# Splitting x1 and h into f16 parts before the transpose instead of after it

## The reference

```
q, k = rope(bf16(x Wq.T)), rope(bf16(x Wk.T))          # one head of 256
o    = sum over the allowed keys of exp(q k.T / 16)    # one number per row
x1   = layernorm(x + relu(o fc1_w.T + fc1_b) fc2_w.T + fc2_b)
```

```
xa = x1 P_w.T                         # 64 numbers per row
C1, C2, C3 = top3_softmax(xa U1.T), top3_softmax(xa U2.T), top3_softmax(xa U3.T)
h  = gelu(sum_e C1[:, e] (x1 W1[e].T))
y  = sum_e C2[:, e] (h W2[e].T) + C3 b2
return layernorm(x1 + y)
```

## Time and profile before

| | |
|---|---|
| median of 3 runs | 327.04 us (326.6 to 327.73) |
| the profiled execution | 327.78 us, of which its span is 325.9 us |
| granted TensorE clock over the span, mean | 0.973 of full speed |
| busy: PE, DVE, ACT, POOL | 284.7, 256.9, 155.6, 115.3 us |
| first mixture of group k's pass 2 starts, k = 0 to 5 | 132.22, 158.42, 184.46, 210.48, 236.52, 262.39 us |
| first mixture of passes 3, 0, 1 and 2 after the one at 184.29 us | 190.92, 197.61, 202.93, 210.32 us |

### The profile page before, as it was taken

The page is one execution under the profiler, slowest core; times in us unless marked ns, Lnnn a source line. Parts: engine busy times, 40 slices in busy tenths (PEclk is TensorE's granted clock), DMA queues, the critical chain, the costliest instruction groups (busy, mean ns, idle before and its releaser), DMA issues.

```text
span 325.9 us, 6342 instructions
## 1 busy us (share of the span) xinstructions
PE 284.7 (87%) x1978; PEld 191.6 (59%) x1978; DVE 256.9 (79%) x849; ACT 155.6 (48%) x327; POOL 115.3 (35%) x264
## 2 busy tenths in 40 slices
PE   0999999979854988999999899899899997999981
PEld 0444455444323667676677577668577566667771
DVE  0069789999976479689889979988988987997672
ACT  1137747655661371435635544634743663634231
POOL 1000018999999102141332431332323314133221
PEclk9999999998995999999999999999999999999997
DMA  8999999700000000000010000000000010010111
GB/s 230 413 411 218 202 187 186 114 2 0 0 1 0 3 2 0 16 20 18 16 35 16 18 16 27 26 18 19 23 27 19 18 32 19 17 34 19 31 33 37
DMA packets 19235, 20.58 MB, mean 63 GB/s; under 512 B 1600, under 2 KB 18432, under 8 KB 18688
## 3 DMA queue, kind: packets, MB, share of 16 engines
q1 hardware_dynamic: 18480, 19.22, 24.2%
q10 hardware_dynamic: 720, 0.93, 1.0%
HBM read 15.94 MB, written 4.19 MB: 62 GB/s over the span
## 4 chain that ended last, share of the span: by engine, by line
PE 35%; DVE 32%; POOL 16%; issue 7%; ACT 6%; DMA 2%; ACTq 0%; DVEq 0%; POOLq 0%
PE bank L830 20%; DVE early L1188 11%; PE bank L686 9%; POOL W L380 5%; POOL wtmp L377 4%; POOL W L379 3%; DVE st L1225 3%; DVE stats L1036 2%; DVE early L1230 2%; POOL rstd L389 2%; DVE top L1057 2%; DMA gatew<-in_gate 2%; ACT x L546 2%; DVE zrest L1068 2%; PE bank L782 2%
## 5 line engine op out<-in xcount | busy, mean ns | idle before, releaser
L830 PE MATMUL bank<-W,early 128*128 (+1 forms) x630 | 75.6, 273 | 6.3 <-DVE early L1188 4.0
L830 PE MATMUL bank<-W,x1T 128*128 (+1 forms) x630 | 77.3, 278 | 0.5 <-DVE early L1188 0.3
L686 PE MATMUL bank<-early,wqk 128*128 128x512 f32 x128 | 65.1, 642 | 8.6 <-DMA gatew<-in_gate 8.6
L830 PEld LDWEIGHTS bank<-W,x1T 128*128 128x128 f16 x630 | 60.5, 99 | 19.9 <-DVE early L1188 9.5
L830 PEld LDWEIGHTS bank<-W,early 128*128 128x128 f16 x630 | 59.5, 98 | 18.2 <-issue 6.0
L1188 DVE SCALAR_TENSOR_TENSOR early<-bank,Csel,early 128x256 f32<-128x256 f32 x124 | 59.4, 479 | 11.6 <-PE bank L830 7.0
L455 POOL TENSOR_SCALAR ve<-mv 128x1 f32<-128x1 f32 x32 | 7.3, 229 | 120.4 <-DVE mv L1226 120.4
L686 PEld LDWEIGHTS bank<-early,wqk 128*128 128x128 f32 x128 | 23.7, 201 | 30.6 <-issue 21.4
L602 ACT ACTIVATE early<-early 128x256 f32<-128x256 f32 x32 | 13.3, 417 | 50.1 <-DVE early L1188 49.9
L497 ACT ACTIVATE qk<-bank 128x512 bf16<-128x512 f32 x32 | 19.0, 594 | 36.7 <-PE bank L686 36.4
L597 ACT ACTIVATE early<-bank,Csel 128x256 f32<-128x256 f32 x31 | 14.6, 472 | 31.0 <-PE bank L830 30.7
(11 more groups left out here) (105 smaller groups left out, 434.0 us busy)
## 6 DMA issues: line engine op xcount, KB each, us to landing
early<-in_xT SPq DMA_DIRECT2D x16, 256.0 KB, 9.4
xs<-in_x SPq DMA_DIRECT2D x32, 128.0 KB, 7.2
out<-early SPq DMA_DIRECT2D x32, 128.0 KB
W<-in_w1T SPq DMA_DIRECT2D x1, 2048.0 KB, 12.1
W<-in_w2T SPq DMA_DIRECT2D x1, 2048.0 KB, 12.3
W<-in_w1T SPq DMA_DIRECT2D x1, 1024.0 KB, 7.7
W<-in_w2T SPq DMA_DIRECT2D x1, 1024.0 KB, 13.8
wqk<-in_wqkT ACTq DMA_DIRECT2D x1, 512.0 KB, 3.9
```

What stands on the lines that cost most here:

```text
L686: mm = pe.matmul(bank[PROJ[n % 2]][:, :], wqk[:, k, g, :], xTb[:, c % 4, k, :, :].rearrange("p s n -> p (s n)"), start=(k == 0), stop=(k = ...
L830: mm = pe.matmul(where[:, 0:DIM], lhs(hx, c), w, start=(k == 0), stop=(k == 5))
```

## The change

The two f16 parts are made in row layout, and the parts are transposed as f16.

- x1: `normed` on ScalarE is followed, after each two tiles, by a cast of these from SBUF into the new tile `xh` (L577 of the changed kernel). `x1_low` becomes a subtraction of two SBUF tiles into `xh`. For groups 0 and 1, in the early stage, VectorE does it; in the main loop GpSimd does (L403), in pass 2 for both halves of the group. TensorE transposes eight f16 blocks instead of four f32 ones (L783). ScalarE copies the bank to `x1T` as 1024 f16 elements per partition (`x1T_copy`, L582) instead of casting 512; nothing is left for VectorE behind the transpose.
- h: after `gelu`, ScalarE casts with the scale into `hh` (`h_high`, L636), and GpSimd scales h in f32 (`hs`, L408) and subtracts (L410) (`h_low`). TensorE transposes four f16 blocks (L960) instead of two f32 ones, and ScalarE copies 512 f16 elements (`hT_copy`, L640). VectorE's L1230 goes.
- TensorE's transpose of h stands behind the side work of its pass instead of ahead of it. On ScalarE `hT_copy` stands behind both parts of the side work.
- GpSimd does `h_low` of tile i-1 ahead of the factors of the final norm of tile i-2, in every pass, and in pass 2 behind `x1_low` of the first half.
- ScalarE makes an f16 identity once (`identh`).

The diff, cut to what differs in the main path:

```diff
...
+        hh = early[:, 2560:3072].bitcast(F16).rearrange("p (r l n) -> p r l n", r=2, l=2)
+        hs = early[:, 3072:3584].rearrange("p (r n) -> p r n", r=2)
...
+            def x1_low(g, h):
+                pool.wait_ge(xhi_done, 2 * g + h + 1)
+                pool.tensor_tensor(xh[:, h, :, 1, :], x1[:, g % 3, 2 * h:2 * h + 2, :], xh[:, h, :, 0, :], ALU.subtract)\
+                    .then_inc(xlo_done, 1)
+
+            def h_low(t):
+                pool.wait_ge(gelu_done, t + 1)
+                link(pool.tensor_scalar(hs[:, t % 2, :], hact[:, t % 2, :], ipow2[:, 1:2], 0.0, ALU.mult, ALU.add))
+                pool.wait_ge(hhi_done, t + 1)
+                pool.tensor_tensor(hh[:, t % 2, 1, :], hs[:, t % 2, :], hh[:, t % 2, 0, :], ALU.subtract).then_inc(hlo_done, 1)
...
-                if (s, pos) == (2, 1) and group(k + 1):
-                    chosen_exps(k + 1)
+                if (s, pos) == (2, 0) and group(k + 2):
+                    x1_low(k + 2, 0)
+                if (s, pos) == (2, 1):
+                    if group(k + 1):
+                        chosen_exps(k + 1)
+                    if group(k + 2):
+                        x1_low(k + 2, 1)
...
                 aux(k, s, 0)
+                if 1 <= i <= NT:
+                    h_low(i - 1)
...
                 n.then_inc(x1_done, 1)
-
-            def x1_high(g, h):
+                act.wait_ge(x1_done, 2 * g + h + 1)
+                wait(act, x1T_done, 2 * (g - 1) + h + 1)
+                act.activation(xh[:, h, :, 0, :], x1[:, g % 3, 2 * h:2 * h + 2, :], ACT.Copy).then_inc(xhi_done, 1)
+
+            def x1T_copy(g, h):
                 act.wait_ge(x1T_done, 2 * g + h + 1)
                 t = GT * g + 2 * h
-                act.activation(x1T[:, t:t + 2, 0, :, :].rearrange("p t c n -> p t (c n)"),
-                               bank[XPOSE][:, :].rearrange("p (t n) -> p t n", t=2), ACT.Copy).then_inc(x1hi_done, 1)
+                act.activation(x1T[:, t:t + 2, :, :, :].rearrange("p t l c n -> p (t l c n)"),
+                               bank[XPOSE][:, :].bitcast(F16), ACT.Copy).then_inc(x1T_copied, 1)
...
+            def h_high(t):
+                act.wait_ge(gelu_done, t + 1)
                 wait(act, hT_done, t - 1)
+                act.activation(hh[:, t % 2, 0, :], hact[:, t % 2, :], ACT.Copy, scale=ipow2[:, 1:2]).then_inc(hhi_done, 1)
+
+            def hT_copy(t):
+                act.wait_ge(hT_done, t + 1)
+                act.activation(hT[:, t % 2, :, :, :].rearrange("p l c n -> p (l c n)"), bank[HT][:, 0:DIM].bitcast(F16),
+                               ACT.Copy).then_inc(hT_copied, 1)
...
                 aux(k, s, 0)
                 if i == 1:
                     begin(1)
+                aux(k, s, 1)
                 if i <= NT:
-                    t = i - 1
-                    act.wait_ge(hT_done, t + 1)
-                    act.activation(hT[:, t % 2, 0, :, :].rearrange("p c n -> p (c n)"), bank[HT][:, 0:DIM], ACT.Copy,
-                                   scale=ipow2[:, 1:2]).then_inc(hhi_done, 1)
-                aux(k, s, 1)
+                    hT_copy(i - 1)
                 if 1 < i < NT:
                     begin(i)
                 if i < NT:
                     gelu(i)
+                    h_high(i)
...
             def x1_transpose(g, h):
-                pe.wait_ge(x1_done, 2 * g + h + 1)
-                wait(pe, x1lo_done, 2 * g + h)
+                pe.wait_ge(xlo_done, 2 * g + h + 1)
+                wait(pe, x1T_copied, 2 * g + h)
...
+                aux(k, s, 1)
                 if i <= NT:
                     t = i - 1
-                    pe.wait_ge(gelu_done, t + 1)
-                    wait(pe, hlo_done, t)
-                    for c in range(NC):
-                        tr = pe.transpose(bank[HT][:, c * P:(c + 1) * P], hact[:, t % 2, c * P:(c + 1) * P], identf[:, :])
+                    pe.wait_ge(hlo_done, t + 1)
+                    wait(pe, hT_copied, t)
+                    for l in range(2):
+                        for c in range(NC):
+                            n = NC * l + c
+                            tr = pe.transpose(bank[HT][:, 0:DIM].bitcast(F16)[:, n * P:(n + 1) * P],
+                                              hh[:, t % 2, l, c * P:(c + 1) * P], identh[:, :])
                     tr.then_inc(hT_done, 1)
-                aux(k, s, 1)
...
             def x1_low(g, h):
-                dve.wait_ge(x1hi_done, 2 * g + h + 1)
-                t = GT * g + 2 * h
-                tiles = x1T[:, t:t + 2, :, :, :].rearrange("p t l c n -> p t l (c n)")
-                dve.tensor_tensor(tiles[:, :, 1, :], bank[XPOSE][:, :].rearrange("p (t n) -> p t n", t=2),
-                                  tiles[:, :, 0, :], ALU.subtract).then_inc(x1lo_done, 1)
+                dve.wait_ge(xhi_done, 2 * g + h + 1)
+                dve.tensor_tensor(xh[:, h, :, 1, :], x1[:, g % 3, 2 * h:2 * h + 2, :], xh[:, h, :, 0, :], ALU.subtract)\
+                    .then_inc(xlo_done, 1)
...
-                if 1 <= i <= NT:
-                    t = i - 1
-                    dve.wait_ge(hhi_done, t + 1)
-                    dve.scalar_tensor_tensor(hT[:, t % 2, 1, :, :].rearrange("p c n -> p (c n)"), bank[HT][:, 0:DIM],
-                                             ipow2[:, 1:2], hT[:, t % 2, 0, :, :].rearrange("p c n -> p (c n)"),
-                                             ALU.mult, ALU.subtract).then_inc(hlo_done, 1)
```

More of the change, by code:

```diff
@@ L1123, in aux @@
             def aux(k, s, pos):
[L1124 to L1128 removed]
+                if (s, pos) == (0, 0) and group(k + 2):
+                    fc_add(k + 2, 0)
                 if (s, pos) == (0, 1) and group(k + 1):
@@ L1144, in aux @@
                     route_mask(k + 1)
-                if (s, pos) == (3, 0):
-                    if group(k):
-                        bias_add(k, 1)
-                    if group(k + 2):
-                        x1_low(k + 2, 0)
+                if (s, pos) == (3, 0) and group(k):
+                    bias_add(k, 1)
                 if (s, pos) == (3, 1) and group(k + 1):
```

54 lines of the change are left out of this document (31 added, 23 removed).

## The result

| | before | after |
|---|---|---|
| median of 4 runs each | 326.82 us (326.04 to 327.73) | 355.65 us (354.81 to 356.29) |
| span of the profiled execution | 325.9 us | 353.3 us |
| granted TensorE clock, mean | 0.973 | 0.958 |

The changed kernel takes 1.088 times as long as the one before, 95% interval 1.0839 to 1.092. The forecast was 352.5 us in a range of 337 to 361.

What follows compares the result with a forecast made beforehand. The prediction took TensorE to bound the main loop, VectorE close behind. It summed 327.8 (this execution) + 17 stall - 0.5 behind the groups + 9 clock = 353.3 us, so 352.5 for the median, range 337 to 361.

Steps and rivals of the forecast that it cites:

- Stall of pass 2: First mixture of pass 1 to that of pass 2 goes from 7.39 to 10.1 us, net 2.7 us more.
- Passes 3, 0 and 1: Pass 3 goes from 6.63 to 7.0 us, pass 0 from 6.69 to 7.1, pass 1 from 5.32 to 5.25.
- Five full groups, 17 us of stall: Groups 1 to 5, between 132.22 and 262.39 us, each take 3.4 us more, 17 us in all.
- The clock: TensorE falls to 1.2 GHz after pass 2's wait, about 1.8 us a group, 9 us in five; bounds 0 and 13.
- Behind the last group: After the five full groups, gains and losses up to the kernel's end come together to about -0.5 us.
- The loop over gelu where no side work covers it: Last passes: the loop over gelu, GpSimd and transpose (4.7 us) is longer than a pass of 4.2, +0.6 us.
- Early stage: Ahead of the main loop, work stays on VectorE and paths stay the same: 0 us, bounds -2 and +2.
- VectorE: Sign of a right forecast: VectorE's busy time over the whole kernel falls to about 234 us.
- rival 4: Pass 2: VectorE's mask and GpSimd's SBUF reads exclude each other, 0.3 us, 1.5 over five groups; not summed, no chance given.
- Rival 1: Main loop: the stall comes without a fall of TensorE's clock, 343.5 us; chance 0.23.
- Rival 3: Main loop: a small loss, a stall of only 1.2 us a group and no clock fall, 333 us; chance 0.10.
- Rival 2: Main loop: VectorE's relief brings `norm_scale` 3.4 us earlier, hides pass 2's chain, kernel faster at 317 us; chance 0.08.

Runs made afterwards that it cites:

- Experiment 2: Changed kernel plus twenty extra matmuls in TensorE's wait ahead of x1's transposes in pass 2 of groups 1 to 5; 349.8 us, ratio 1.071.
- experiment 4: Changed kernel with everything of h put back as in the kernel before, so only x1 is split in rows; 336.56 us (332.54 to 339.53).
- experiment 7: Changed kernel with the edits of Experiment 1 and experiment 5, x1's first-half transposes a pass later, `normed`'s second half behind `begin` in pass 2; 322.47 us, ratio 0.9867.
- experiment 10: The kernel of experiment 7 with all of h's part taken back to the kernel before; 318.91 us, ratio 0.9748.
- experiment 3: Changed kernel with x1's split and f32 transpose put back as in the kernel before, so only h is in rows; 338.78 us, ratio 1.0334.
- Experiment 1: Changed kernel with h's low part ahead of the low part of x1's first half on GpSimd in pass 2; 353.42 us, ratio 1.0796.
- experiment 5: Changed kernel with the gate product ahead of x1's transposes in pass 3 and router logits in pass 0, ScalarE's C3 copy ahead of x1's; 345.49 us, ratio 1.0574.
- experiment 8: The kernel of experiment 3 with the gate product ahead of x1's transposes in pass 3 and ahead of the logits in pass 0; 330.32 us, ratio 1.0103.

## Why the prediction was right

The direction, the size and the mechanism held: 353.3 us was forecast for the profiled execution and 355.1 came. By its own steps:

- **Stall of pass 2.** First mixture of pass 1 to that of pass 2: 10.1 us forecast, 9.62 measured (215.58 to 225.20), so 2.23 more than before instead of 2.7. The chain itself was right: 4.69 us from ScalarE's x to the mixture, 4.71 forecast (5.06 without the 0.35 of the final norm). Its steps differ by little: 1.15 us for the low part of x1 (1.21 taken), 0.67 for h's subtraction (0.69), 0.53 for its scaling (0.47). What was off is where it starts: x comes 0.84 us sooner behind the first mixture of pass 1 (4.92 instead of 5.76), where the working had 0.35, since `shift` is ready 1.04 us sooner instead of 0.7 and the final norm delays x by 0.20 instead of 0.35. Between the bias product and the mixture lie 4.2 us, not 4.9. Waits of 2.58 and 0.64 us stand where 3 and 1 were named.
- **Passes 3, 0 and 1.** Forecast 7.0, 7.1 and 5.25; measured 8.58 less the 1.5 of the slow mixture, so 7.1, then 7.39 and 5.31. In pass 0 one link was overlooked: the small copy of C3's transpose (0.26 us) stands behind the 1.00 us copy on ScalarE, and TensorE waits for the semaphores of both. The copy itself had been put at 1.0 us. ScalarE's work grew by 4.6 us per group (the working's four terms add up to 4.4, not the 4.5 it gives), GpSimd's by 6.8 instead of 7.1.
- **Five full groups, 17 us of stall:** 17.1. That it is so close is luck: pass 2 came out 0.5 us shorter and passes 3 and 0 some 0.4 longer.
- **The clock.** Five falls were expected and five came. Forecast 1.8 us each; the slow mixtures cost 1.3 to 1.7, 7.2 in all instead of 9. Experiment 2 shows it by adding work. The length taken from the earlier trace rows, 3.5 us at 1.2 GHz, was right: here it is 3.4. The comparison with the 2.1 idle microseconds ahead of the second fall of the earlier trace rows was a weak ground: at the same place the changed kernel fell 3.4 us after its last work (94.95 to 98.35), and in experiment 4 equal waits ended both ways. Whether the transposes ahead of the mixture count for the clock, which the prediction left open, no run isolates.
- **Behind the last group.** Forecast -0.5, measured 3.0, of which 1.3 is the fifth fall, which the forecast had counted with the clock. Of the other 1.7, group 5's last half is +0.45 (forecast +0.5), VectorE's relief in group 6 is -1.1 (-1.7), the last h 0 (+0.3). The loop over gelu where no side work covers it is the term that was too small: +2.3 instead of +0.6, of which 1.2 stand in one pass, at 322.22. The last group's passes show it (timeline), against the earlier trace rows:

```profile
322.22 0.40 PE L960 MATMUL bank<-identh,early 128*128 128x128 f16 x4 [1.12 <-POOL early L410]
...
343.06 0.40 PE L960 MATMUL bank<-identh,early 128*128 128x128 f16 x4 [0.50 <-POOL early L410]
```

- **Early stage.** Forecast 0 within 2 us, measured 1.4. TensorE comes to the first product of tile 0 at 103.00 instead of 102.26, and the clock, low since 98.35, is back in the half microsecond from 108.5 instead of 106.5. What makes it late was not tested.
- **VectorE.** 234 us busy was forecast, 243.3 measured. The routers' mask shows what was left out (least, median and most in ns, changed kernel, then the kernel before):

```profile
L1119 DVE TENSOR_TENSOR mask<-zs,zrest x8: 290/926/933, 89.5 to 312.3; 128x144 bf16<-128x144 f32 x8
```

```profile
L1075 DVE TENSOR_TENSOR mask<-zs,zrest x8: 295/298/300, 89.1 to 287.6; 128x144 bf16<-128x144 f32 x8
```

It starts at 253.53, inside GpSimd's low part of x1 (253.14 to 254.29), and ends 0.17 us behind it. It cost the path nothing, since TensorE was waiting anyway. The mask's rows add up to 5.5 us instead of 2.4, which is 3 us of the 9. Another 2 are the four low parts of x1 that VectorE makes in the early stage, 4.8 us for what took 2.8; the rest I have not followed up. By the Trainium skill, SBUF — State Buffer, Who interferes with whom, a VectorE instruction with two SBUF inputs contends with a GpSimd one that reads SBUF, and who issues first keeps the port. The rows agree in both: GpSimd was first and kept its 1.15 us, as long as its second low part at 257.26, which had no mask beside it. The forecast's rival 4 had named this place, and had the wrong engine lose.

**The rivals.** Rival 1 (no fall of the clock) fails by the windows at 255.5 and by experiment 2. Rival 3 (a stall of 1.2 us a group) fails by the 3.4 us measured. Rival 2, that VectorE's relief wins, was wrong for this order of instructions: `shift` came 1.04 us sooner, not the 3.4 it needed. Experiments 7 and 10 take the chain off the path by where it stands, not by starting it sooner, and come to 322.5 and 318.9 us. They don't show that VectorE's relief is what pays: experiment 10 keeps less of it than experiment 7 and is faster.

**What the forecast did not price** is h's part alone, which costs 11.7 us (experiment 3). The working had its two links in passes 3 and 0, the cast of h on ScalarE and TensorE's arrival 0.4 us earlier; it was experiment 3's expectation that took the part as free. x1's part alone costs 9.5 us by the median of experiment 4, whose executions lie 7 us apart, and both together 28.8, which is 7.6 more than the sum. The groups without a fall show where. h alone makes them 0.95 us longer, x1 alone 0.83, both 3.4. Passes 3 and 0 add up (1.54 and -0.38 give the 1.15 measured). Pass 1 to 2 doesn't: -0.57 and +1.23 would be 0.66, and it is 2.23, so 1.6 us a group, 8 in five. Experiment 1, which takes h's low part from behind x1's on GpSimd, gives back 0.98 of the 1.6. Where the other 0.6 lies no run shows. The falls of the clock are not the difference: two in each part alone cost 6.7 us in slow mixtures, five in the changed kernel 7.2.

## What to carry to other kernels

Before work is handed to an idle engine, write down the chain that it lengthens and what TensorE does meanwhile; x1's added links cost 1.2 us in pass 2 where they stood ahead of its mixture (experiment 4) and nothing where they ran beside it (experiment 10). Look as well at what a new instruction stands in front of: ScalarE's cast of h cost 0.53 us in each of two passes because another chain waited behind it (experiment 3). An instruction that depends on nothing late is worth more ahead of a wait than behind it (experiments 5 and 8), and one that is moved away from a wait costs its full length where it goes (0.23 us in experiment 3). Price a stall of TensorE with the lower clock that may follow it: here the mixture behind a stall of 2.2 to 3.2 us was 0.7 to 1.9 us longer wherever the clock fell.

## What the runs showed of the hardware

- Two waits of the same 2.21 us, between the same instructions of one execution, were followed once by full clock and once by the lower one (experiment 4). The time of such a kernel is not settled by its instructions alone: its executions ranged from 332.54 us at a mean clock of 0.981 to 339.53 at 0.948.
- The clock stayed low for two different lengths: 3.4 us in all five falls of the changed kernel, with a mixture of 3.46 to 3.79 us behind, and 6.8 us in three falls of experiment 1 (189.4 to 196.2, 250.8 to 257.7 and 281.5 to 288.4 us), with a mixture of 4.05 us. In these three it fell while TensorE waited, 0.8 to 1.3 us ahead of the transposes of x1.
- Eight f16 transposes of 128 columns take TensorE about as long as four f32 ones: 0.46 us from 208.10 to the next matmul at 208.56 in experiment 10, and 0.49 us in the earlier trace rows.
- ScalarE's copy of 1024 f16 elements out of PSUM took 1.00 us, that of 512 0.58 to 0.60.
